# The inner layer of a four-bit feed-forward: another order of the work on TensorE and ScalarE

## The chip, the core and the metric

The kernel runs on one core of a Trainium2 chip. Five engines work from queues of their own and meet only at semaphores: TensorE (PE, matmuls and transposes, writes to PSUM), VectorE (DVE), ScalarE (ACT), GpSimd (POOL) and SyncE (SP, which issues DMAs). The metric is the device time of one launch in microseconds; lower is better. An engine works off its queue in the order in which the program wrote it: an instruction that waits for a semaphore holds up all that stand behind it on that engine, and none on another.

## The reference, cut to what matters

The model is two hybrid layers on a tensor x of shape 8 x 512 x 128. The feed-forward touched here, `_L0_ffn_ref`, is used twice, after each of the first two mixing blocks:

```python
xq   = fp4_quant_dequant(layernorm(x))          # blocks of 16 along the features
gate = einsum('bsk,nk->bsn', xq, fp4(w_gate))   # 128 -> 352
y    = einsum('bsk,nk->bsn', xq, fp4(w_up))     # 128 -> 352
h    = silu(gate) * y
x    = x + einsum('bsk,nk->bsn', fp4_quant_dequant(h), fp4(w_down))   # 352 -> 128
```

`fp4_quant_dequant` scales each block of 16 values so that its largest magnitude is 6, rounds each value to the nearest of 0, 0.5, 1, 1.5, 2, 3, 4, 6 with its sign, and multiplies by the scale again.

## The kernel before, in words

`ffn0_stages` (line 649) runs two stages per call and is called twice. The first, "fx", normalises and quantises x into `XQ`. The second, "fh" (line 795), is the one changed; in the profile its tiles are named `fh_...`. It treats G = 32 tiles j of 128 tokens; two tiles make a pair k (16 pairs), and four tiles, NT = 4, make one block m of 512 tokens (8 blocks). All tiles are f32. One pass of it takes about 115 us, and there are two passes, from 479 to 594 us and from 751 to 871 us of the span.

What happens to one tile, with the line of each instruction:

- TensorE: gate (line 822) into one of two PSUM buffers `gps`; up (line 826) into one of four buffers `ups`. Gate j may start when the silu of tile j-2 has been read out (`s.gt`), up j when `total` of tile j-4 is done (`s.tot`).
- ScalarE: `gated`, the silu of the gate (line 863).
- VectorE: `product` (line 888), `maxima` of the blocks of 16 (line 892), `scales` for the pair (lines 898 and 900), `scaled` (line 904).
- ScalarE: the magnitude times 2^22, called size (line 873).
- VectorE: `sizes` for the pair (line 909), which is the number to round against, and `total` (line 913). Adding that number to the value is what rounds it.
- GpSimd: subtracts it again (`q`, line 942) and multiplies by the scale (`hq`, line 945).
- TensorE: `turn`, three transposes of the tile (line 833) into the single buffer `tps`. ScalarE copies it out in two pieces (lines 879 and 880) to `HT`; the next turn waits for both copies (`s.ht`).
- TensorE: `down` (line 841), after the four tiles of a block have been turned: three f32 matmuls of 512 columns into the single buffer `yps`. It waits for the copies, and for VectorE to have added the previous block's result to X (`s.x`, lines 932 and 935).

Every f32 matmul appears in the profile as two MATMUL records, except a transpose, which appears as one.

The order on each engine is written out by hand. VectorE's cycle for pair k is: the products of pair k, `sizes` and both totals of pair k-1, the maxima, scales and scaled of pair k, and in every second cycle from k = 5 the addition of a finished block to X. TensorE and ScalarE go by single tiles before the change. In TensorE's cycle j come gate j+2, up j+2, turn j-4 (LAG = 4), and after every fourth turn `down`. In ScalarE's cycle j come the silu of tile j+2, the size of tile j, and the two copies of tile j-4.

Of the kernel before, what the change touches and what calls it, by code (L numbers as in the profile page):

```python
# [10 lines left out]
ACT = mybir.ActivationFunctionType  # L11
AX_X = mybir.AxisListType.X

P = 128
# [3 lines left out]
NT = T // P  # L18
N_STATE = 16
FF = 352  # L20
# [20 lines left out]
STEP = 2.0 ** 22  # L41
# [607 lines left out]
def ffn0_stages(nc, w, X):  # L649
# [7 lines left out]
    with Stage(nc, "ffn") as outer:  # L657
        XQ = outer.sb("xq", [P, B, T])
        with Stage(nc, "fx") as st:
# [8 lines left out]
            size, mag, tot, q, xq = ([st.sb(f"{n}{k}", [P, NB, FQ]) for k in range(2)] for n in ("size", "mag", "tot", "q", "xq"))  # L668
            s = st.sems("cent sq lnv rough var v1 v2 rstd amax normed above inv both xn size mag tot q xq back out")
            with st.block() as block:  # L670

                @block.tensor
                def _(pe):
                    def center(k):
                        pe.wait_ge(s.tot, max(k - RING + 1, 0))
                        for t in range(TOK):
                            n, at = 2 * k + t // NT, t % NT * P
                            m = pe.matmul(cps[k % RING][:, t * XB:(t + 1) * XB, :].rearrange("p a q -> p (a q)"), X[:, n, at:at + P], w.center[:, :], start=True, stop=True)
                        m.then_inc(s.cent, 1)

                    def back(k):
                        pe.wait_ge(s.xq, k + 1)
                        for j in range(2):
                            pe.wait_ge(s.out, max(2 * k + j - 1, 0))
                            for t in range(NT):
                                a = (j * NT + t) * XB
                                m = pe.transpose(qps[j][:, t * P:(t + 1) * P], xq[k % 2][:, a:a + XB, :].rearrange("p a q -> p (a q)"), w.ident[:, :])
                            m.then_inc(s.back, 1)

                    center(0)  # L690
                    center(1)
                    for k in range(PAIRS):
                        if k + 2 < PAIRS:
                            center(k + 2)
                        back(k)
# [98 lines left out]

        with Stage(nc, "fh") as st:
            G = NT * B
            LAG = 4
            gps = [st.ps(f"g{k}", [P, FF]) for k in range(2)]
            ups = [st.ps(f"u{k}", [P, FB, FQ]) for k in range(4)]
            tps = st.ps("t", [P, KF, P])  # L800
            yps = st.ps("y", [P, T])
            gt, q, hq = ([st.sb(f"{n}{k}", [P, FB, FQ]) for k in range(NT)] for n in ("gt", "q", "hq"))
            size, mag, tot = ([st.sb(f"{n}{k}", [P, 2, FB, FQ]) for k in range(2)] for n in ("size", "mag", "tot"))
            amax, above, inv = ([st.sb(f"{n}{k}", [P, 2, FB]) for k in range(4)] for n in ("amax", "above", "inv"))
            HT = [st.sb(f"ht{k}", [P, KF, T]) for k in range(2)]
            s = st.sems("g u gt h amax above inv xn size mag tot q hq t ht y x")
            flat = "p a q -> p (a q)"

            def real(j):

                return 0 <= j < G

            with st.block() as block:

                @block.tensor
                def _(pe):
                    def tokens(j):
                        return XQ[:, j // NT, j % NT * P:(j % NT + 1) * P]

                    def gate(j):  # L820
                        pe.wait_ge(s.gt, max(j - 1, 0))
                        pe.matmul(gps[j % 2][:, :], tokens(j), w.gate[:, :], start=True, stop=True).then_inc(s.g, 1)

                    def up(j):
                        pe.wait_ge(s.tot, max(j - 3, 0))
                        pe.matmul(ups[j % 4][:, :, :].rearrange(flat), tokens(j), w.up[:, :], start=True, stop=True).then_inc(s.u, 1)

                    def turn(j):
                        pe.wait_ge(s.hq, j + 1)
                        pe.wait_ge(s.ht, 2 * j)  # L830
                        for c in range(KF):
                            cols = min(P, FF - c * P)
                            i = pe.transpose(tps[0:cols, c, :], hq[j % NT][:, c * P // FQ:(c * P + cols) // FQ, :].rearrange(flat), w.ident[:, :])
                        i.then_inc(s.t, 1)

                    def down(m):
                        pe.wait_ge(s.ht, 2 * NT * (m + 1))
                        pe.wait_ge(s.x, m)
                        for c in range(KF):
                            rows = min(P, FF - c * P)  # L840
                            i = pe.matmul(yps[:, :], w.down[0:rows, c, :], HT[m % 2][0:rows, c, :], start=(c == 0), stop=(c == KF - 1))
                        i.then_inc(s.y, 1)

                    gate(0)
                    gate(1)
                    up(0)
                    up(1)
                    for j in range(G + LAG + 1):
                        if real(j + 2):
                            gate(j + 2)  # L850
                            up(j + 2)
                        k = j - LAG
                        if real(k):
                            turn(k)
                        if k >= NT and k % NT == 0:
                            down(k // NT - 1)

                @block.scalar
                def _(act):
                    def gated(j):  # L860
                        act.wait_ge(s.g, j + 1)
                        act.wait_ge(s.h, max(j - NT + 1, 0))
                        act.activation(gt[j % NT][:, :, :].rearrange(flat), gps[j % 2][:, :], ACT.Silu).then_inc(s.gt, 1)

                    gated(0)
                    gated(1)
                    for j in range(G + LAG):
                        if real(j + 2):
                            gated(j + 2)
                        if real(j):  # L870
                            act.wait_ge(s.xn, j + 1)
                            act.wait_ge(s.mag, max(j // 2 - 1, 0))
                            act.activation(size[j // 2 % 2][:, j % 2, :, :], ups[j % 4][:, :, :], ACT.Abs, scale=STEP).then_inc(s.size, 1)  # L873
                        k = j - LAG
                        if real(k):
                            m, t = divmod(k, NT)
                            act.wait_ge(s.t, k + 1)
                            act.wait_ge(s.y, max(m - 1, 0))
                            act.activation(HT[m % 2][:, 0:2, t * P:(t + 1) * P], tps[:, 0:2, :], ACT.Copy).then_inc(s.ht, 1)
                            act.activation(HT[m % 2][0:FF - 2 * P, 2, t * P:(t + 1) * P], tps[0:FF - 2 * P, 2, :], ACT.Copy).then_inc(s.ht, 1)  # L880

                @block.vector
                def _(dve):
# [1328 lines left out]
```

## Time and profile before

| what | before |
|---|---|
| median of 3 runs | 2394.18 us (2393.65 to 2394.51) |
| the profiled execution | 2391.51 us, its span 2389.5 us |
| mean granted TensorE clock | 0.921 |
| TensorE, matmul busy | 1911.1 us, 80% |
| VectorE busy | 1571.5 us, 66% |
| ScalarE busy | 1375.2 us, 58% |
| GpSimd busy | 1019.3 us, 43% |
| stage fh, both passes | 479 to 594 us and 751 to 871 us |

The span is the part of an execution in which the core works; the execution's own time is 2.0 us longer. Busy shares are means over stages that have different limits, so the change has to be judged from the two stretches in which stage fh runs. The granted clock is a share of 2.4 GHz; 0.5 in a stretch stands for 1.2 GHz throughout.

### The profile page before, as it was taken

How to read it: one execution, taken by the hardware profiler on the slowest of the kernel's cores; microseconds unless marked ns; L12 is line 12 of the kernel's file. 1: busy time of each engine (PE TensorE's matmuls, PEld its weight loads, DVE VectorE, ACT ScalarE, POOL GpSimd, SP SyncE). 2: the span in 40 equal slices, each digit the busy share in tenths (PEclk: the TensorE clock that was granted, in tenths of full speed). 3: DMA queues.
4: the chain of work that ended last, by engine and by line, in shares of the span. 5: the costliest groups of instructions: out<-in, count | busy, mean ns of one | idle time of the engine just before them, and what ended most of it. 6: DMA issues, size and time to landing. Idle time of an engine off the chain costs nothing. (4 is left out here: it accounts for less than half of the span.)

```text
span 2389.5 us, 36303 instructions
## 1 busy us (share of the span) xinstructions
PE 1911.1 (80%) x11731; PEld 865.0 (36%) x11731; DVE 1571.5 (66%) x2373; ACT 1375.2 (58%) x2286; POOL 1019.3 (43%) x1118
## 2 busy tenths in 40 slices
PE   4457886377774765899999999999999966599997
PEld 2113332243453421344444444444444422222222
DVE  4979995786447856777777777777777635511112
ACT  2446662343333334677666676666666533599995
POOL 0156663244004521466666666666666631500001
PEclk9769998589896987999999999999999988899999
DMA  2000000000000001111111111111111100512110
GB/s 87 0 14 0 0 0 0 1 1 1 0 1 0 1 1 52 47 55 54 53 54 56 56 56 56 56 56 56 56 56 56 50 24 8 124 41 52 46 50 36
DMA packets 71431, 84.45 MB, mean 35 GB/s; under 512 B 20545, under 2 KB 44033, under 8 KB 71169
## 3 DMA queue, kind: packets, MB, share of 16 engines
q1 hardware_dynamic: 66224, 79.80, 11.5%
q10 hardware_dynamic: 5040, 2.56, 0.4%
q8 instruction: 90, 1.47, 0.3%
q14 instruction: 77, 0.62, 0.1%
HBM read 71.95 MB, written 9.57 MB: 34 GB/s over the span
## 5 line engine op out<-in xcount | busy, mean ns | idle before, releaser
L1638 DVE SCALAR_TENSOR_TENSOR fu_kv<-fu_ps_kv,fa_vec,fu_kv 128x511 f32<-128x511 f32 x366 | 253.2, 741 | 5.6 <-ACT fu_kv L1568 4.0
L2032 ACT ACTIVATE rt_p<-rt_ps_s 128x1024 f32<-128x1024 f32 x256 | 240.3, 1042 | 25.3 <-PE rt_ps_o L1977 16.5
L1716 POOL TENSOR_TENSOR fu_p<-fu_p 128x768 f32<-128x768 f32 x64 | 116.2, 1816 | 295.2 <-PE fu_ps_n L1413 290.8
L1383 PE MATMUL fu_ps_s<-fu_qn,fu_kn 64*128 64x512 f32 (+3 forms) x1024 | 190.0, 468 | 6.1 <-ACT fu_p L1550 5.5
L1618 DVE TENSOR_REDUCE fu_nm<-fu_ps_m 128x2 f32<-128x1024 f32 x64 | 78.4, 1225 | 176.5 <-PE fu_ps_m L1406 176.5
L602 POOL TENSOR_TENSOR scan_hC<-scan_h,scan_c 128x1024 f32<-128x1024 f32 x64 | 150.7, 2354 | 82.9 <-DVE scan_h L582 82.9
L1413 PE MATMUL fu_ps_n<-fu_p,fu_vt 128*64 128x512 f32 (+3 forms) x1024 | 166.1, 445 | 0.0
L527 PE MATMUL scan_ps_y<-scan_hC,w_ident 128*128 128x512 f32 x256 | 130.3, 632 | 40.9 <-POOL scan_hC L602 24.3
L582 DVE TENSOR_TENSOR_SCAN scan_h<-scan_dA,scan_ps_b 128x1024 f32<-128x1024 f32 x64 | 146.4, 2287 | 2.2
L1977 PE MATMUL rt_ps_o<-rt_p,rt_va 128*32 128x512 f32 x1024 | 137.2, 608 | 10.0 <-ACT rt_p L2032 8.1
L1441 PE MATMUL fu_ps_kv<-w_XN,fa_wp 128*128 128x512 f32 x244 | 122.8, 626 | 17.3 <-DVE fu_cr L1611 15.3
L1383 PEld LDWEIGHTS fu_ps_s<-fu_qn,fu_kn 64*128 64x128 f32 x1024 | 82.9, 185 | 125.3 <-ACT fu_p L1572 52.1
L1966 PE MATMUL rt_ps_s<-ra_stackq,ra_stackk 48*128 48x512 bf16 x512 | 94.4, 391 | 24.6 <-PEq L73 15.5
L563 ACT ACTIVATE scan_c<-scan_ps_c 128x1024 f32<-128x1024 f32 x64 | 65.5, 1023 | 75.3 <-POOL scan_hC L602 46.3
L942 POOL TENSOR_TENSOR fh_q<-fh_tot,fh_mag 128x352 f32<-128x352 f32 x64 | 59.4, 928 | 111.3 <-DVE fh_tot L913 111.3
L1568 ACT ACTIVATE fu_kv<-fu_ps_kv,fa_vec 128x512 f32<-128x512 f32 x122 | 80.6, 686 | 38.2 <-PE fu_ps_kv L1441 34.8
L1954 POOL COPY rt_va<-ra_v 128x128 f32<-128x128 f32 x32 | 8.0, 293 | 220.3 <-PE rt_ps_o L1977 220.2
L1656 DVE SCALAR_TENSOR_TENSOR fu_og<-fu_num,fu_ow,fu_ro 128x512 f32<-128x512 f32 x64 | 84.2, 1316 | 14.4 <-issue 6.0
L559 ACT ACTIVATE scan_dA<-ssm_delta,w_decay 128x511 f32 (+1 forms) x128 | 85.0, 713 | 12.3 <-DVE scan_dA L574 11.4
L1758 POOL TENSOR_TENSOR fu_num<-fu_num,fu_sg 128x512 f32<-128x512 f32 x64 | 81.3, 1271 | 22.6 <-DVE fu_sg L1681 19.4
L873 ACT ACTIVATE fh_size<-fh_ps_u 128x352 f32<-128x352 f32 x64 | 29.9, 467 | 101.6 <-DVE fh_ps_u L904 101.6
L1574 ACT ACTIVATE fu_p<-fu_ps_s 128x512 f32<-128x512 f32 x64 | 38.2, 597 | 86.5 <-PE fu_ps_s L1391 86.5
(353 smaller groups left out, 5071.3 us busy)
## 6 DMA issues: line engine op xcount, KB each, us to landing
fu_rb<-rms_rows SPq DMA_DIRECT2D x256, 128.0 KB, 3.0
fu_ro<-rms_rows SPq DMA_DIRECT2D x128, 128.0 KB, 3.0
ra_stackq<-rope_parts SPq DMA_DIRECT2D x168, 32.0 KB
ra_stackk<-rope_parts SPq DMA_DIRECT2D x168, 32.0 KB
w_X<-in_xT SPq DMA_DIRECT2D x4, 512.0 KB
fa_wp<-in_wp SPq DMA_DIRECT2D x8, 256.0 KB
fu_cr<-ncum_rows SPq DMA_DIRECT2D x128, 3.0 KB
rope_parts<-rp_hi SPq DMA_DIRECT2D x16, 128.0 KB, 2.9
```

The costliest lines, as they stand in the source:

```text
L527: i = pe.matmul(yps[:, :], w.ident[:, :], hC[p % (BEHIND + 2)][:, j, :], start=(p == 0 and j == 0), stop=(p == PAIRS - 1 and j == 1))
L559: m = act.activation(dA[p % 2][:, j, 1:T], DL[:, n, 1:T], ACT.Exp, scale=w.decay[:, k:k + 1])
L582: dve.tensor_tensor_scan(flat[0], flat[1], flat[2], 0.0, ALU.mult, ALU.add).then_inc(s.scan, 1)
L602: pool.tensor_tensor(hC[p % (BEHIND + 2)][:, :, :], hst[p % 2][:, :, :], csb[p % 2][:, :, :], ALU.mult).then_inc(s.hC, 1)
L1383: pe.matmul(sps[:, h, at:at + T - t * P], k[head(h), t * P:(t + 1) * P], q[head(h), t * P:T], start=(at == 0), stop=False)
L1413: m = pe.matmul(nps[head(h), t * P:T], VT[b % VR][:, t, head(h)], p[:, h, :], start=(t == 0), stop=(t == 2))
L1441: pe.matmul(projected(a, j), wp[:, g, 1 + j, :], XN[:, n, :], start=True, stop=True).then_inc(s.kvp, 1)
L1638: dve.scalar_tensor_tensor(acc, projected(a, k)[:, 0:T - j], vec[:, a % GA, at:at + 1], acc, ALU.mult, ALU.add).then_inc(done, 1)
L1716: pool.tensor_tensor(tail, tail, P13[:, :, 0:3 * P], ALU.add).then_inc(s.d1, 1)
L1966: m = pe.matmul(sps[u % RING][:, e, :], stack[1][rows, 2 * q4 + i, t * P:(t + 1) * P], stack[0][rows, 2 * q4 + i, :], start=True, stop=True)
L1977: m = pe.matmul(ops[32 * j:32 * j + 32, :], va[:, t, 4 * q4 + j, :], pr[k % 2][j // 2][:, j % 2, :], start=(t == 0), stop=(t == NT - 1))
L2032: act.activation(pr[k % 2][i][:, :, :], sps[(U * n + u) % RING][:, :, :], ACT.Exp, scale=DH_B ** -0.5).then_inc(s.exp, 1)
```

## The change

TensorE and ScalarE are written in pairs of tiles, as VectorE already was, and LAG becomes 2 and counts pairs; turns therefore still come four tiles behind.

- TensorE's cycle k: for each of two tiles first its turn (of pair k-2), then its up (of pair k+1); then both gates of pair k+2; then, in every second cycle, `down`.
- ScalarE's cycle k: the two silus of pair k+1, the four copies of pair k-2, the two sizes of pair k.
- VectorE, GpSimd, all buffers, all waits and all instructions as such are the same; only their places in TensorE's and ScalarE's queues differ.

```diff
--- before.py
+++ after.py
@@ -794,7 +794,7 @@
 
         with Stage(nc, "fh") as st:
             G = NT * B
-            LAG = 4
+            LAG = 2
             gps = [st.ps(f"g{k}", [P, FF]) for k in range(2)]
             ups = [st.ps(f"u{k}", [P, FB, FQ]) for k in range(4)]
             tps = st.ps("t", [P, KF, P])
@@ -841,19 +841,20 @@
                             i = pe.matmul(yps[:, :], w.down[0:rows, c, :], HT[m % 2][0:rows, c, :], start=(c == 0), stop=(c == KF - 1))
                         i.then_inc(s.y, 1)
 
-                    gate(0)
-                    gate(1)
-                    up(0)
-                    up(1)
-                    for j in range(G + LAG + 1):
-                        if real(j + 2):
-                            gate(j + 2)
-                            up(j + 2)
-                        k = j - LAG
-                        if real(k):
-                            turn(k)
-                        if k >= NT and k % NT == 0:
-                            down(k // NT - 1)
+                    for j in range(2):
+                        gate(j)
+                        up(j)
+                    for k in range(-1, G // 2 + LAG):
+                        for e in range(2):
+                            if real(2 * (k - LAG) + e):
+                                turn(2 * (k - LAG) + e)
+                            if k >= 0 and real(2 * k + 2 + e):
+                                up(2 * k + 2 + e)
+                        for e in range(2):
+                            if real(2 * k + 4 + e):
+                                gate(2 * k + 4 + e)
+                        if k > LAG and (k - LAG) % 2 == 1:
+                            down((k - LAG) // 2)
 
                 @block.scalar
                 def _(act):
@@ -862,22 +863,23 @@
                         act.wait_ge(s.h, max(j - NT + 1, 0))
                         act.activation(gt[j % NT][:, :, :].rearrange(flat), gps[j % 2][:, :], ACT.Silu).then_inc(s.gt, 1)
 
-                    gated(0)
-                    gated(1)
-                    for j in range(G + LAG):
-                        if real(j + 2):
-                            gated(j + 2)
-                        if real(j):
-                            act.wait_ge(s.xn, j + 1)
-                            act.wait_ge(s.mag, max(j // 2 - 1, 0))
-                            act.activation(size[j // 2 % 2][:, j % 2, :, :], ups[j % 4][:, :, :], ACT.Abs, scale=STEP).then_inc(s.size, 1)
-                        k = j - LAG
-                        if real(k):
-                            m, t = divmod(k, NT)
-                            act.wait_ge(s.t, k + 1)
-                            act.wait_ge(s.y, max(m - 1, 0))
-                            act.activation(HT[m % 2][:, 0:2, t * P:(t + 1) * P], tps[:, 0:2, :], ACT.Copy).then_inc(s.ht, 1)
-                            act.activation(HT[m % 2][0:FF - 2 * P, 2, t * P:(t + 1) * P], tps[0:FF - 2 * P, 2, :], ACT.Copy).then_inc(s.ht, 1)
+                    def sized(j):
+                        act.wait_ge(s.xn, j + 1)
+                        act.wait_ge(s.mag, max(j // 2 - 1, 0))
+                        act.activation(size[j // 2 % 2][:, j % 2, :, :], ups[j % 4][:, :, :], ACT.Abs, scale=STEP).then_inc(s.size, 1)
+
+                    def turned(j):
+                        m, t = divmod(j, NT)
+                        act.wait_ge(s.t, j + 1)
+                        act.wait_ge(s.y, max(m - 1, 0))
+                        act.activation(HT[m % 2][:, 0:2, t * P:(t + 1) * P], tps[:, 0:2, :], ACT.Copy).then_inc(s.ht, 1)
+                        act.activation(HT[m % 2][0:FF - 2 * P, 2, t * P:(t + 1) * P], tps[0:FF - 2 * P, 2, :], ACT.Copy).then_inc(s.ht, 1)
+
+                    for k in range(-1, G // 2 + LAG):
+                        for part, j in ((gated, 2 * k + 2), (turned, 2 * (k - LAG)), (sized, 2 * k)):
+                            for e in range(2):
+                                if real(j + e):
+                                    part(j + e)
 
                 @block.vector
                 def _(dve):
```

## Rows read from the trace of the kernel before

**Rows 1.** Busy time by stretch: from:to, us, each engine's busy us, PEclk, DMA share, GB/s.

```profile
488.59:512.10 23.51, 17.99 (x56) 9.65 (x56) 20.72 (x44) 9.14 (x28) 13.56 (x16) 0.85 0.00 1
...
524.55:581.10 56.55, 39.60 (x140) 21.53 (x140) 48.34 (x102) 22.42 (x68) 30.47 (x36) 0.95 0.00 1
581.10:594.10 13.00, 9.45 (x25) 4.33 (x24) 2.33 (x4) 2.72 (x10) 3.38 (x4) 0.81 0.00 0
...
761.02:784.52 23.50, 17.07 (x56) 9.39 (x56) 20.70 (x44) 9.14 (x28) 13.54 (x16) 0.93 0.00 1
784.52:858.55 74.03, 53.99 (x174) 29.08 (x174) 59.18 (x125) 27.75 (x84) 37.22 (x44) 0.89 0.00 1
858.55:871.06 12.51, 8.97 (x25) 4.12 (x24) 2.32 (x4) 2.72 (x10) 3.38 (x4) 0.84 0.00 1
```

**Rows 2.** Timeline of VectorE: start us, us, engine, line, instruction [idle before <-releaser].

```profile
512.10 0.95 DVE L913 TENSOR_TENSOR fh_tot<-fh_mag,fh_ps_u 128x352 f32<-128x352 f32 x2
...
515.91 0.68 DVE L932 TENSOR_TENSOR w_X<-w_X,fh_ps_y 128x512 f32<-128x512 f32 x1
516.50 0.95 DVE L888 TENSOR_TENSOR fh_ps_u<-fh_gt,fh_ps_u 128x352 f32<-128x352 f32 x2
517.37 0.52 DVE L909 TENSOR_SCALAR fh_mag<-fh_size 128x704 f32<-128x704 f32 x1
517.92 0.95 DVE L913 TENSOR_TENSOR fh_tot<-fh_mag,fh_ps_u 128x352 f32<-128x352 f32 x2
...
520.85 0.96 DVE L904 TENSOR_TENSOR fh_ps_u<-fh_ps_u,fh_inv 128x352 f32<-128x352 f32 x2
521.72 0.52 DVE L888 TENSOR_TENSOR fh_ps_u<-fh_gt,fh_ps_u 128x352 f32<-128x352 f32 x1
523.55 0.53 DVE L888 TENSOR_TENSOR fh_ps_u<-fh_gt,fh_ps_u 128x352 f32<-128x352 f32 x1 [1.31 <-PE fh_ps_u L826]
...
524.55 0.95 DVE L913 TENSOR_TENSOR fh_tot<-fh_mag,fh_ps_u 128x352 f32<-128x352 f32 x2
```

**Rows 3.** Timeline of TensorE's matmuls in the same twelve microseconds.

```profile
518.49 0.86 PE L826 MATMUL fh_ps_u<-w_up,ffn_xq 128*128 128x352 f32 x2 [0.74 <-DVE fh_tot L913]
...
519.19 0.49 PE L833 MATMUL fh_ps_t<-w_ident,fh_hq 128*128 128x128 f32 x3
...
519.52 2.74 PE L841 MATMUL fh_ps_y<-fh_ht,w_down 128*128 128x512 f32 x6
...
522.10 0.76 PE L822 MATMUL fh_ps_g<-w_gate,ffn_xq 128*128 128x352 f32 x2
...
522.69 0.75 PE L826 MATMUL fh_ps_u<-w_up,ffn_xq 128*128 128x352 f32 x2
...
523.28 0.49 PE L833 MATMUL fh_ps_t<-w_ident,fh_hq 128*128 128x128 f32 x3
```

**Rows 4.** Timeline of ScalarE and GpSimd in the same stretch.

```profile
521.27 0.79 POOL L945 TENSOR_TENSOR fh_hq<-fh_q,fh_above 128x352 f32<-128x352 f32 x1
521.42 0.46 ACT L873 ACTIVATE fh_size<-fh_ps_u 128x352 f32<-128x352 f32 x1 [3.16 <-DVE fh_ps_u L904]
...
523.81 0.38 ACT L879 ACTIVATE fh_ht<-fh_ps_t 128x256 f32<-128x256 f32 x1
...
524.09 0.26 ACT L880 ACTIVATE fh_ht<-fh_ps_t 96x128 f32<-96x128 f32 x1
```

**Rows 5.** The line that forms the scales: durations ns min/median/max, first and last start.

```profile
L898 DVE TENSOR_SCALAR fh_above<-fh_amax x32: 186/583/592, 485.5 to 855.1; 128x44 f32<-128x44 f32 x32
```

**Rows 6.** A VectorE stall at half clock, and the down projection's durations (tile view).

```profile
L841 PE MATMUL fh_ps_y<-fh_ht,w_down x96: 590/593/1061, 507.1 to 869.7; 128*128 128x512 f32 x64, 96*128 96x512 f32 x32
...
562.33 0.53 DVE L888 TENSOR_TENSOR fh_ps_u<-fh_gt,fh_ps_u 128x352 f32<-128x352 f32 x1 [2.76 <-PE fh_ps_u L826]
```

**Rows 7.** The end of the first pass, timeline.

```profile
590.52 2.85 PE L841 MATMUL fh_ps_y<-fh_ht,w_down 128*128 128x512 f32 x6 [0.64 <-ACT fh_ht L880]
593.40 0.69 DVE L935 TENSOR_TENSOR w_X<-w_X,fh_ps_y 128x512 f32<-128x512 f32 x1 [5.61 <-PE fh_ps_y L841]
```

## The prediction

> **What bounds the kernel now.** I began with the page's 40 slices to place stage fh, then cut both passes by VectorE's totals (line 913), which mark its cycles: T(1) to T(16) are the starts of the first total in cycles 1 to 16, 15 intervals. They take 23.51 us for four, 12.45 for the next two and 56.55 for nine in pass 1, 92.51 in all, and 23.50 + 74.03 = 97.53 in pass 2; the rest up to the last addition is 13.00 and 12.51 [rows 1, 2]. In the 56.55 us VectorE is busy 48.34, TensorE 39.60, GpSimd 30.47 and ScalarE 22.42 [rows 1]. So VectorE is nearly the bound, and the question is what it waits for. The reader is to see in its timeline two kinds of cycle. One, with an addition to X, runs without a gap: 512.10 to 517.92 is 5.82. The other takes 6.63 (517.92 to 524.55), and its second product sat idle for 1.31 us until an up matmul ended [rows 2]. TensorE's timeline says why: `down` stood in the queue ahead of gate and up, from 519.52 to the next gate at 522.10 [rows 3]. Nothing in the stretch runs beside something else's end: both passes lie in series with the stages around them, so what they lose or win shows in full.
>
> **VectorE's own floor.** Its instructions and their order are not touched, so the new cycle can be put together from gapless pieces. From total to scaled 2.93 (517.92 to 520.85), scaled to product 0.87, two products to sizes 0.87 (516.50 to 517.37), sizes to total 0.55: 5.22, taken as 5.23. An addition puts 0.59 in (515.91 to 516.50), and 5.82 is what was measured [rows 2]. The last interval has an addition and no products, so ScalarE's size ends it: about 5.0. Additions stand in cycles 5, 7, 9, 11, 13 and 15. Fifteen intervals: 9 x 5.23 + 5 x 5.82 + 5.0 = 81.2 us. Against 92.5 and 97.5 that is 11.3 and 16.3 us, if no other engine ever comes late. That is what has to be checked, engine by engine.
>
> **Does TensorE come late?** Start to start at the full clock: gate or up 0.59 (522.10, 522.69, 523.28), three transposes 0.33 (519.19 to 519.52), down 2.58 (519.52 to 522.10) [rows 3]. Two cycles need 4 x 0.33 + 8 x 0.59 + 2.58 = 8.6 us of the floor's 11.05, so it has room. The places: a waiting up starts 0.57 after the total (517.92 to 518.49) [rows 2, 3]. In an odd cycle (T its total): up T+0.57, turn 1.16, up 1.49, gates 2.08 and 2.67, free at 3.26. Now `down`. It waits for the previous block's addition, which stands at T+3.80 in the same VectorE cycle and lasts 0.68: down starts at T+4.53, not 3.26. This wait is harmless in the old order and is met in the new one in cycles 5, 7, ... 15. Behind it in the queue stand the next turn and up. They get TensorE at T+4.53+2.58 = T+7.11, which is 1.29 us into the next cycle (T'). From there: turn 1.29, up 1.62; the second turn needs both copies of the first. Turn to copy is 0.53, copy to copy 0.28, the second lasts 0.26 [rows 3, 4], and with about 0.15 for the signal the second turn starts at T'+2.51, the second up at 2.84 and ends at 2.84+0.75 = 3.6 [rows 3]. VectorE wants the first tile at T'+3.80 and the second at T'+4.23. So the up is in time by 0.6 us, and before it was late by 1.31. The gates follow at T'+3.4 and 4.0 for silus that are wanted a whole cycle later; two pairs ahead, they can no longer make the product wait. The 0.6 us is the thinnest cover in the change on this engine: longer down, turns or copies by more than that come back one for one, six or seven times a pass.
>
> **Does ScalarE come late?** VectorE's sizes needs both magnitudes by T'+4.66. The first starts 0.57 after scaled (520.85 to 521.42), at T'+3.50 [rows 2, 4], the second 0.43 later; it lasts 0.46 and ends at 4.4, 0.25 us early. In the even cycle the second tile's copies end at about T'+3.6 (turn 2.51, then the 1.07 above), just when the first size could start, which eats some 0.1 of the 0.25. Everything else on ScalarE has microseconds. GpSimd needs 4.14 us after a total until both tiles are out (521.27 + 0.79, from 517.92) of a cycle of 5.23 [rows 4], and a turn wants them a cycle later. No DMA, SyncE instruction or buffer is involved.
>
> **A contention that could move.** The scales instruction of 128 x 44 elements takes 583 ns at the median and 186 at least, the first of a pass, when GpSimd is still idle [rows 5]. Both start from the total, and stay in the same phase in the new order, so I keep the 583; 0.4 us per cycle below that would need GpSimd elsewhere. The Trainium skill (GPSIMD Engine Reference, section Specifications) says that GpSimd's SBUF interfaces are shared with VectorE and contended by instructions in a two-port mode. By that rule a closer cycle would speak against the change if the 704-element sizes came to lie beside GpSimd. The trace's phases answer it: sizes at T+4.66, GpSimd done at T+4.14, so by the rule and by the row the sum is the same, with 0.5 us of margin.
>
> **Clock.** The stretches were granted 0.95 and 0.89 of full speed [rows 1]. A stall that fell at half clock was 2.76 instead of 1.31 [rows 6]. TensorE idles 12.45 - 8.6 = 3.8 us per two cycles now and 2.4 in the new order, in pieces of 0.3, 0.9 and 1.3. I take full clock in the loop, and count falls in the range: one lengthens the chain behind down by what the two stalls differ by, 2.76 - 1.31 = 1.45 us, less the 0.6 of cover, so costs about 0.9.
>
> **Start and end.** The second product still waits for the first two gates and ups, whatever their order, so I count the start at nothing. At the end, before, `down` of block 6 ran after the last totals, in front of four turns. Now it starts at T(15)+4.53, 0.5 us ahead of T(16). But TensorE has stood idle for some four microseconds by then (no up and no gate is left in cycle 15, and by the working above the second turn is done 5 to 5.5 us after T(14), down starts 9.8 after it), and half-clock matmuls of down last 1061 ns instead of 593 [rows 6], so it may run to T(16)+3.9. Then three turn intervals of 1.24, 1.15 from turn to down, 2.88 down to addition (590.52 to 593.40), 0.69 [rows 7]: 12.3. With the full clock it is about 10.5, the last tile from GpSimd at T(16)+4.14 then being the limit. I take 12.3: 0.7 and 0.2 us gained; the other end is 2.5 and 2.0.
>
> **Sum.** 11.3 + 16.3 + 0.7 + 0.2 = 28.5 us. Profiled execution 2391.5 - 28.5 = 2363.0. The runs shown have their median 2.7 above the profiled one, so 2365.7.
>
> **Rivals.**
>
> *A. The wait for the addition leaves a stall.* The chain addition, down, turn, two copies, turn, up has six signals, and I priced each from one row. If they add 1 to 2 us, VectorE still waits 0.4 to 1.4 us in every even cycle, 6 a pass, 12 in all: 5 to 17 us back, time 2371 to 2383, about 2376. For it: 0.6 us is thin, and this wait was never met in the trace of before. Against it: every link is in a row, and the old chain is regular to 0.01 us.
>
> *B. The size comes late.* If the copies of the second turn run into the sizes by 0.3 us more than I have, sizes waits 0.15 to 0.3 in the even cycles and the 0.46 us silu in front of it comes to matter: 12 to 28 cycles by 0.2 is 2 to 6 us, about 2370.
>
> *C. Slower, by the clock.* TensorE now stands idle 1.3 us right ahead of its longest work, and again 0.9. If the clock stays at 1.2 GHz there, down takes 5.16, the turns and up double, and the second product comes at about T'+7.7 instead of 4.23: 3.5 us in each of 12 even cycles, 42 us, more than the loops' 27.6 that the order brings. That gives 2366 + 42 = 2408. It decides as soon as two of three chains run at half clock (27.6 / 42). Against it: before, the idle pieces were longer and the clock was 0.95 and 0.89. The Trainium skill (TensorE: Matmul & The Clock Gate, section A second HAM failure mode) describes a kernel in which frequent short idles between groups of matmuls make the clock go up and down; by that rule falls would not vanish here. The trace shows such falls, at most in a part of the stalls.
>
> *D. No change.* The wait would have to move whole to another engine; the work of ScalarE and GpSimd, 22.42 and 30.47 of 56.55, speaks against it [rows 1].
>
> **How the numbers follow.** Forecast 0.66, A 0.14, B 0.12, C 0.04, D 0.02, and 0.02 for a gain above the range, from a vanished contention or both tails at full clock. Forecast alone: 2361 (tails at full clock, 28.5 + 3.6 = 32.1, and a little more) to 2370 (five falls of the clock at 0.9 us). With A's likelier half the range is 2360 to 2378. About 0.2%, 4.8 us, is what a measurement of this kernel can tell from no change. Faster 0.94 (forecast, B, A, the extra), same 0.02, slower 0.04.
>
> **What would show it.** In the trace after: VectorE's intervals from total to total alternating 5.23 and 5.82 with no product waiting for up; down starting about 0.06 us after line 932's addition ends, and not with the last gate; size (line 873) directly behind scaled for both tiles, 0.43 apart; the 15 intervals 81 us in both passes, alike. Idle before line 888 of over 0.1 us in even cycles says A; idle before line 909 says B; down records above 1 us in the loop say C.

## The result and the profile after

The changed kernel takes 2370.41 us (median of 4 runs, 2367.84 to 2371.97) against 2393.91 us before (4 runs, 2392.79 to 2394.51): a ratio of 0.9900, with a 95% interval of 0.9886 to 0.9914. The forecast was 2365.7 us, with 2360 to 2378 as its range. The profiled execution took 2367.84 us, its span 2366.0, against 2391.51 and 2389.5.

| from the profiled executions, us | before | forecast | after |
|---|---|---|---|
| pass 1: first gate to T(1) | 9.56 | 9.56 | 8.86 |
| pass 1: 15 intervals | 92.51 | 81.2 | 81.80 |
| pass 1: end | 12.99 | 12.3 | 16.24 |
| pass 2: first gate to T(1) | 9.69 | 9.69 | 9.56 |
| pass 2: 15 intervals | 97.53 | 81.2 | 80.97 |
| pass 2: end | 12.51 | 12.3 | 12.76 |
| both passes | 234.8 | 206.3 | 210.2 |

Here and below an interval runs from the first total of one VectorE cycle to that of the next, and the end of a pass from T(16) to the end of its last addition. Both passes together became 24.6 us shorter and everything else 1.1 us longer, which makes the span's 23.5.

The stretches of the changed kernel, each pass's 15 intervals and its end, which answer to [rows 1] (columns as there):

```profile
488.29:570.09 81.80, 63.55 (x229) 35.77 (x230) 79.11 (x170) 36.97 (x112) 50.77 (x60) 0.97 0.00 1
570.09:586.33 16.24, 12.71 (x24) 4.90 (x23) 2.32 (x4) 2.18 (x8) 3.38 (x4) 0.64 0.00 0
753.20:834.17 80.97, 63.56 (x229) 35.71 (x230) 78.90 (x170) 37.00 (x112) 50.75 (x60) 0.96 0.00 1
834.17:846.93 12.76, 9.22 (x24) 3.78 (x23) 2.33 (x4) 2.18 (x8) 3.38 (x4) 0.85 0.00 1
```

VectorE is now busy 79.11 of 81.80 us: it has become the bound of the loop. Its timeline, an even cycle and an odd one (... stands for rows left out), beside [rows 2]:

```profile
526.82 0.95 DVE L915 TENSOR_TENSOR fh_tot<-fh_mag,fh_ps_u 128x352 f32<-128x352 f32 x2
...
530.62 0.95 DVE L890 TENSOR_TENSOR fh_ps_u<-fh_gt,fh_ps_u 128x352 f32<-128x352 f32 x2
...
532.04 0.95 DVE L915 TENSOR_TENSOR fh_tot<-fh_mag,fh_ps_u 128x352 f32<-128x352 f32 x2
...
535.83 0.68 DVE L934 TENSOR_TENSOR w_X<-w_X,fh_ps_y 128x512 f32<-128x512 f32 x1
536.43 0.95 DVE L890 TENSOR_TENSOR fh_ps_u<-fh_gt,fh_ps_u 128x352 f32<-128x352 f32 x2
...
537.84 0.95 DVE L915 TENSOR_TENSOR fh_tot<-fh_mag,fh_ps_u 128x352 f32<-128x352 f32 x2
```

The two products of a cycle follow each other in one record, with no idle time in front of either: 5.22 and 5.80 us. Two rows of the table remain to be read, the ends. Both `down` of the end of pass 1 are here, then both of pass 2:

```profile
569.73 5.46 PE L841 MATMUL fh_ps_y<-fh_ht,w_down 128*128 128x512 f32 x6 [4.13 <-DVE w_X L934]
...
574.98 0.56 PE L833 MATMUL fh_ps_t<-w_ident,fh_hq 128*128 128x128 f32 x3
...
580.25 5.35 PE L841 MATMUL fh_ps_y<-fh_ht,w_down 128*128 128x512 f32 x6 [0.63 <-ACT fh_ht L876]
585.64 0.69 DVE L937 TENSOR_TENSOR w_X<-w_X,fh_ps_y 128x512 f32<-128x512 f32 x1 [9.73 <-PE fh_ps_y L841]
...
833.81 4.86 PE L841 MATMUL fh_ps_y<-fh_ht,w_down 128*128 128x512 f32 x6 [4.14 <-DVE w_X L934]
...
843.36 2.85 PE L841 MATMUL fh_ps_y<-fh_ht,w_down 128*128 128x512 f32 x6 [0.63 <-ACT fh_ht L876]
```

TensorE stood idle for 4.13 us ahead of `down` of block 6 and ran it in 5.46 us, at half clock; in pass 1 the last `down` came at half clock as well (5.35 against 2.85), and the mean granted clock of that end is 0.64.

Below, each experiment's median stands beside runs of the kernel before that were measured together with it, and kernels are compared by these ratios; a pair of figures in brackets is the lowest and highest run, or, behind a ratio, its 95% interval.

### The profile page after: what moved, and what is told of

Read it like the earlier page. It is cut to its first block and busy times, and to the rows that moved or that the text cites. A ratio compares the mean times of both kernels' runs of the same rounds, so it can differ in the third digit from the quotient of the medians.

```text
span 2366.0 us, 36303 instructions
## 1 busy us (share of the span) xinstructions
PE 1907.3 (81%) x11731; PEld 863.8 (37%) x11731; DVE 1564.1 (66%) x2373; ACT 1375.2 (58%) x2286; POOL 1021.3 (43%) x1118
## 3 DMA queue, kind: packets, MB, share of 16 engines
q8 instruction: 90, 1.47, 0.3%
## 5 line engine op out<-in xcount | busy, mean ns | idle before, releaser
L1968 PE MATMUL rt_ps_s<-ra_stackq,ra_stackk 48*128 48x512 bf16 x512 | 94.7, 393 | 24.6 <-PEq L73 15.5
L535 PE MATMUL scan_ps_b<-ssm_bc,scan_selbc 96*128 (+1 forms) x128 | 40.7, 401 | 56.9 <-DMA scan_selbc<-in_selbc 56.3
```

Source lines behind the costliest of these rows:

```text
L1968: m = pe.matmul(sps[u % RING][:, e, :], stack[1][rows, 2 * q4 + i, t * P:(t + 1) * P], stack[0][rows, 2 * q4 + i, :], start=True, stop=True)
```

## Experiments

**1. TensorE's order alone.** ScalarE keeps its order by single tiles (silu of j+2, size of j, copies of j-4).

```diff
-                    for k in range(-1, G // 2 + LAG):
-                        for part, j in ((gated, 2 * k + 2), (turned, 2 * (k - LAG)), (sized, 2 * k)):
+                    for j in range(G + 4):
+                        # silu of j + 2, size of j, copies of j - 4, as before
```

> TensorE in the new order, ScalarE in the old one by single tiles. Theory (the two orders need each other: the second turn of a pair stands in front of the second up, and waits for the first turn's copies): in the old order ScalarE makes those copies only behind the size of the pair's first tile, T+3.9 to 4.4, so turn comes at T+4.5 and the up ends at T+5.6 instead of T+3.6; a cycle from total to total is then about 6.65 us instead of 5.23 or 5.82, the 15 intervals of a pass about 100 us (before 92.5 and 97.5, after 81.8 and 81.0), and the time about 2404 us, slower than before. Rival (moving down to the end of TensorE's cycle and the gates ahead is what brings the gain, ScalarE's order adds the 0.3 to 0.5 us of late sizes in cycles without an addition): about 2378 us.

2417.92 us (2414.16 to 2421.16) beside 2393.02, ratio 1.0108 (1.0081 to 1.0134). The 15 intervals take 105.7 and 104.9 us, about half of them 6.75 or 7.68. ScalarE's, TensorE's and VectorE's timeline in one of 6.80, close to the first kind:

```profile
525.21 0.46 ACT L874 ACTIVATE fh_size<-fh_ps_u 128x352 f32<-128x352 f32 x1 [2.92 <-DVE fh_ps_u L905]
...
525.61 0.39 ACT L880 ACTIVATE fh_ht<-fh_ps_t 128x256 f32<-128x256 f32 x1
525.89 0.26 ACT L881 ACTIVATE fh_ht<-fh_ps_t 96x128 f32<-96x128 f32 x1
...
526.30 0.52 PE L833 MATMUL fh_ps_t<-w_ident,fh_hq 128*128 128x128 f32 x3
...
526.65 0.76 PE L826 MATMUL fh_ps_u<-w_up,ffn_xq 128*128 128x352 f32 x2
...
527.52 0.53 DVE L889 TENSOR_TENSOR fh_ps_u<-fh_gt,fh_ps_u 128x352 f32<-128x352 f32 x1 [0.72 <-PE fh_ps_u L826]
```

That is the chain expected: the size, then the copies, the second turn, the second up, and only then the product. The 6.75 was expected as 6.65; the intervals of 7.5 and more were not, and with them the time is 14 us above the 2404 expected. They come with a mean clock of 0.85 in the loop; that the clock alone makes them was not tested. The rival (2378) falls.

**2. ScalarE's order alone.** TensorE keeps gate, up, turn by single tiles, with `down` after every fourth turn.

```diff
-                    for k in range(-1, G // 2 + LAG):
-                        # turn, up, turn, up; both gates; down
+                    for j in range(G + 4 + 1):
+                        # gate and up of j + 2, turn of j - 4, down, as before
```

> ScalarE in the new order, TensorE in the old one by single tiles with down in the middle. Theory (the orders need each other): the silus and copies of both tiles stand in front of the sizes, and the second gate and second turn come late, behind down above all; sizes end about T+5.2 in cycles with an addition or without down, and T+7.9 in those with down, so intervals of about 5.8 and 8.4 us, 107 us a pass, about 2415 us, clearly slower than before. Rival (late sizes were half of the matter, and ScalarE's order alone takes them away): a little faster than before, about 2388 us, with the stall of the second product behind down still 1.3 us.

2426.84 us (2425.48 to 2428.41) beside 2393.02, ratio 1.0147 (1.0123 to 1.0171). Intervals of 6.9 and 10.1 us in pass 1 (116.3 for 15), of about 7.0 and 8.4 in pass 2 (110.1): the 8.4 was expected, the 6.9 to 7.0 had been put at 5.8, and the 10.1 comes with a lower clock again (0.82 against 0.87) and five `down` of 3.9 to 4.1 us where pass 2 has 2.74. In a cycle of pass 1 with `down`:

```profile
518.96 3.89 PE L841 MATMUL fh_ps_y<-fh_ht,w_down 128*128 128x512 f32 x6
...
523.48 0.46 ACT L863 ACTIVATE fh_gt<-fh_ps_g 128x352 f32<-128x352 f32 x1 [6.90 <-PE fh_ps_g L822]
...
524.14 0.53 DVE L889 TENSOR_TENSOR fh_ps_u<-fh_gt,fh_ps_u 128x352 f32<-128x352 f32 x1 [3.00 <-PE fh_ps_u L826]
...
526.36 0.53 DVE L910 TENSOR_SCALAR fh_mag<-fh_size 128x704 f32<-128x704 f32 x1 [1.69 <-ACT fh_size L868]
```

ScalarE, which now does nothing else before the second silu, waits 6.90 us for its gate behind `down`, and VectorE waits twice. So each half alone makes the kernel slower, by 1.1 and 1.5%, and the two together 1.0% faster: they are one change, and there is no share of the gain for either.

**3. Down in front of the gates.** Only TensorE's `down` moves, to between the ups and the gates.

```diff
+                        if k > LAG and (k - LAG) % 2 == 1:
+                            down((k - LAG) // 2)
                         for e in range(2):
                             if real(2 * k + 4 + e):
                                 gate(2 * k + 4 + e)
-                        if k > LAG and (k - LAG) % 2 == 1:
-                            down((k - LAG) // 2)
```

> The changed kernel with down in front of the two gates of its cycle instead of behind them. Theory (last in the cycle matters because down waits for the addition until T+4.5 and holds up whatever stands behind it): the gates come at T'+2.5, the silus behind them hold back the first turn's copies and the sizes, and the even cycles grow by about 2.2 us, five a pass, so the time is about 2392 us; at least 0.6 us a cycle, 2376 us. Rival (gates are wanted a whole cycle later, so their place is free): 2370 us, intervals unchanged.

2387.32 us (2380.79 to 2390.61) beside 2393.02, ratio 0.9977 (0.9965 to 0.9989): most of the gain is gone. The 15 intervals take 94.0 and 94.8 us; after a `down` that waits for an addition they are 7.99 in nine of ten. Forecast was 2.2 us more than 5.22, or 7.4. What was missing:

```profile
526.07 4.51 PE L841 MATMUL fh_ps_y<-fh_ht,w_down 128*128 128x512 f32 x6 [2.27 <-DVE w_X L934]
...
530.42 1.35 PE L822 MATMUL fh_ps_g<-w_gate,ffn_xq 128*128 128x352 f32 x4
...
531.21 1.06 ACT L864 ACTIVATE fh_gt<-fh_ps_g 128x352 f32<-128x352 f32 x2 [5.37 <-PE fh_ps_g L822]
...
532.80 0.53 DVE L890 TENSOR_TENSOR fh_ps_u<-fh_gt,fh_ps_u 128x352 f32<-128x352 f32 x1 [1.65 <-PE fh_ps_u L826]
...
534.07 0.53 DVE L890 TENSOR_TENSOR fh_ps_u<-fh_gt,fh_ps_u 128x352 f32<-128x352 f32 x1 [0.74 <-PE fh_ps_u L826]
```

Without the gates to do, TensorE idles 2.27 us until the addition instead of 1.09, and `down` then takes 4.51 us instead of 2.8, mostly at half clock. The first such `down` of pass 1 had the same 2.27 us of idle time ahead of it and still took 2.82; the interval after it is the tenth, 6.30. So the idle time alone does not say whether the clock falls.

**4. The gates one pair ahead.** They stand first in TensorE's cycle, in front of the turns and ups.

```diff
+                        for e in range(2):
+                            if k >= 0 and real(2 * k + 2 + e):
+                                gate(2 * k + 2 + e)
                         # turn, up, turn, up as before
-                        for e in range(2):
-                            if real(2 * k + 4 + e):
-                                gate(2 * k + 4 + e)
```

> The changed kernel with the gates one pair ahead instead of two: they stand first in TensorE's cycle, just before the turns and ups of the same cycle. Theory (two pairs ahead takes the silus, and the copies behind them, off the chain behind down): after a down, gates come at T'+1.3 and 1.9, the first turn's copies wait for the second silu until T'+3.1, the second up ends at T'+4.9 against 4.2, and the sizes end at 5.7 against 4.7: 0.7 to 1.05 us in each of five even cycles a pass, 7 to 10 us, about 2379 us; intervals after a down of 5.9 to 6.3 instead of 5.22. Rival (the pairing alone carries the gain, gates are early enough one pair ahead): intervals unchanged, 2370 us.

2389.58 us (2385.79 to 2392.43) beside 2395.44, ratio 0.9975 (0.9965 to 0.9986), 94.0 us for the 15 intervals in both passes, and 7.99 again in eight of ten (6.29 in the others). I had overlooked that this is the same queue as in experiment 3: `down`, both gates, turn. "Gates two pairs ahead" and "down last" are one statement, and this run repeats the one above; the 5.9 to 6.3 us expected left the clock out.

**5. Is it the place or the clock?** Experiment 3, with three matmuls that nobody reads in each of the five waits of a pass for the addition:

```diff
                         pe.wait_ge(s.ht, 2 * NT * (m + 1))
+                        for i in range(3 if 0 < m < B - 2 else 0):
+                            pe.matmul(tps[:, :, :].rearrange("p c o -> p (c o)")[:, 0:FF], w.ident[:, :], w.gate[:, :], start=True, stop=True)
                         pe.wait_ge(s.x, m)
```

> Down in front of the gates and the additions where they were, with three matmuls of 352 columns, whose results nobody reads, in each of the five waits of a pass for the addition (blocks 1 to 5). Theory (the cycles of 7.99 us are made of the place, 1.1 us, and of down at half clock behind 2.3 us of idle time, 1.7 us): down runs at full clock and the intervals after it become 6.3 us, 15 of them about 87 us instead of 94 to 95, about 2374 us. Rival (the clock has no part, it is the place alone): intervals of 7.99 stay, 2387 us.

2377.44 us (2375.20 to 2377.88) beside 2393.78, ratio 0.9927 (0.9907 to 0.9947). Every interval after a waiting `down` is 6.23, the 15 take 86.95 and 86.09. TensorE's timeline (line 839 is the three unread matmuls):

```profile
523.55 2.04 PE L839 MATMUL fh_ps_t<-w_gate,w_ident 128*128 128x352 f32 x6
525.69 2.85 PE L843 MATMUL fh_ps_y<-fh_ht,w_down 128*128 128x512 f32 x6
528.37 1.35 PE L822 MATMUL fh_ps_g<-w_gate,ffn_xq 128*128 128x352 f32 x4
```

So of the 2.77 us (7.99 - 5.22) the place costs 1.01 and the half clock behind the idle time 1.76. With more work on TensorE the kernel is faster than in experiment 3 (ratio 0.9927 against 0.9977).

**6. Down in front of the gates, without its wait.** Experiment 3 with VectorE's additions moved from the odd cycles to the even ones (the start of the closing loop, which adds what is left, changes with it and is left out here):

```diff
-                        if k >= 5 and k % 2 == 1:
+                        if k >= 4 and k % 2 == 0:
```

> Down in front of the gates, and the additions moved to the even cycles, so that down no longer waits for one. Theory (down's place matters only through that wait: behind it TensorE stands idle 2.3 us when the gates come after down, against 1.1 to 1.3 when they come before): intervals of 5.22 and 5.82 in both passes, 82 us for 15, as with the additions moved alone, about 2366 us. Rival (down's 2.6 us in front of the gates are too much for the cycle whatever it waits for): even cycles above 6 us remain, 2375 us or more.

2363.36 us (2361.05 to 2368.45) beside 2393.78, ratio 0.9878 (0.9856 to 0.9900). The 15 intervals take 81.87 and 81.85 us, in 5.22 and 5.82 but for one of 6.1 in each pass, behind `down` of block 0:

```profile
485.56:567.43 81.87, 66.51 (x238) 36.66 (x238) 79.19 (x169) 38.03 (x114) 50.84 (x60) 0.98 0.00 1
```

With no wait for the addition `down` may stand on either side of the gates; its place matters through that wait alone.

**7. The changed kernel with the additions in even cycles.** The same edit of VectorE's queue in the changed kernel.

> The changed kernel, with VectorE's additions of a finished block moved by one cycle, from the odd cycles 5, 7, ... to the even ones 4, 6, ...; down then finds its wait for the previous addition already met and starts with the last gate at T+3.3. Theory (in the loop the wait for the addition is covered; it costs only at the end of a pass, where it puts down of block 6 behind 4 us of idle time, at half clock): the 15 intervals stay at 81 us in both passes, the end of a pass falls from 16.2 and 12.8 to about 9.0 to 11.5 us, time about 2364 us. Rival (the wait costs in the loop too): the intervals fall by over 1 us a pass. Rival (no effect, the end is set by the last tile alone): 2370 us.

2367.60 us (2366.96 to 2370.16) beside 2393.02, ratio 0.9896 (0.9873 to 0.9919):

```profile
488.18:570.04 81.86, 65.19 (x238) 37.25 (x238) 79.18 (x170) 37.62 (x114) 50.89 (x60) 0.98 0.00 1
570.04:581.99 11.95, 7.79 (x15) 3.05 (x15) 2.23 (x4) 1.63 (x6) 3.38 (x4) 0.56 0.00 0
750.50:832.35 81.85, 66.68 (x237) 37.76 (x237) 79.16 (x169) 37.08 (x112) 50.87 (x60) 0.96 0.00 1
832.35:843.00 10.65, 6.29 (x17) 2.54 (x15) 2.23 (x4) 2.18 (x8) 3.40 (x4) 0.84 0.00 1
```

The loop doesn't gain by it: the wait for the addition was covered, as forecast. (Pass 2 took 0.9 us more, by one interval of 6.05 behind `down` of block 0.) The ends fall by 4.3 and 2.1 us. The run's time shows none of it, 0.9896 against 0.9900: in these two profiles the forgetting attention stage, which the edit does not touch, took 1041.7 us here and 1035.6 in the changed kernel.

**8. The ends of a pass, filled.** The changed kernel with ten gate matmuls that nobody reads (the expectation says nine): six before `down` of block 6, one each before turns 29, 30 and 31 and the last `down`. The places from which it is called are left out here.

```diff
+                    def filler(n):
+                        pe.wait_ge(s.gt, G)
+                        for i in range(n):
+                            pe.matmul(gps[i % 2][:, :], tokens(0), w.gate[:, :], start=True, stop=True)
```

> The changed kernel with nine more gate matmuls, whose results nobody reads, put where TensorE stands idle at the end of a pass: six in front of down of block 6, one each in front of turns 29, 30 and 31 and of the last down. Theory (the end of a pass is long because both downs run at half clock behind idle time): both run at full clock, down records near 0.59 us, and the end falls from 16.2 and 12.8 to about 10.6 us in both passes, time about 2362 us. Rival (the waits set the end, the clock does not matter): the ends stay, or grow by the fillers, 2370 to 2373 us.

2363.31 us (2363.28 to 2366.31) beside 2391.89, ratio 0.9880 (0.9860 to 0.9900). Both ends:

```profile
569.09:579.82 10.73, 9.57 (x32) 4.22 (x30) 2.33 (x4) 2.18 (x8) 3.39 (x4) 1.00 0.00 0
827.65:838.38 10.73, 9.56 (x32) 4.22 (x30) 2.33 (x4) 2.18 (x8) 3.39 (x4) 1.00 0.00 1
```

10.73 us at a clock of 1.00, where 16.24 and 12.76 had been at 0.64 and 0.85. Filled ends with the additions in even cycles, here eight matmuls: one before turn 29, four before turn 30, two before turn 31 and one before the last `down`:

> The additions moved to even cycles as before, and eight filler matmuls at the end of a pass (one before turn 29, four before turn 30, two before turn 31, one before the last down). Theory of the clock: the last down runs at full clock, ends of 11.95 and 10.65 us become about 9.2 in both passes, time about 4 us below the same kernel without fillers (2367.6), 2363 us. Rival (fillers stand in the way of the turns): ends of 11 us or more.

2359.82 us (2354.16 to 2363.01) beside 2391.89, ratio 0.9857 (0.9833 to 0.9880), ends of 8.95 and 9.84 us at 1.00, where 9.2 was expected. In pass 2 `down` of block 6, which stands ahead of T(16) here and has no filler in front, took 4.43 us instead of 2.84.

**9. The scales instruction.** The block maxima go to unused columns of PSUM buffers of the tiles (`ups`). The lines that write and read them are left out here.

```diff
-            ups = [st.ps(f"u{k}", [P, FB, FQ]) for k in range(4)]
+            uraw = [st.ps(f"u{k}", [P, 32, FQ]) for k in range(4)]
+            ups = [u[:, 0:FB, :] for u in uraw]
+            amax = [uraw[2 * k][:, 24:27, :].rearrange("p a q -> p (a q)")[:, 0:2 * FB].rearrange("p (t f) -> p t f", f=FB) for k in range(2)]
```

> The changed kernel, with the block maxima kept in PSUM beside the tile that they come from instead of in SBUF; the scales instruction of 128 x 44 elements then reads PSUM. Theory (its 583 ns instead of 186 is a contention with GpSimd for SBUF): it falls to about 0.2 us, the interval without an addition from 5.22 to about 4.83, with some 0.2 us given back in even cycles, where the sizes then end last (0.17 us of cover so far): about 9 to 11 us in all, 2360 us. Rival (the 0.4 us is a latency of the short chain itself, or PSUM costs as much): the instruction stays near 0.58, intervals unchanged, 2370 us.

2354.77 us (2351.89 to 2357.44) beside 2391.89, ratio 0.9840 (0.9819 to 0.9861), more than the 9 to 11 us expected: the loops became 9.4 us shorter (76.66 and 76.75 for 15 intervals), and the ends 3.7 (12.42 and 12.84). These are the usual ends of this order, as experiment 11 shows, and the 3.7 us are not put down to the instruction. The instruction in the changed kernel and, below it, in this one (durations min/median/max):

```profile
L900 DVE TENSOR_SCALAR fh_above<-fh_amax x32: 185/582/592, 485.3 to 831.0; 128x44 f32<-128x44 f32 x32
```

```profile
L902 DVE TENSOR_SCALAR fh_above<-fh_ps_u x32: 203/204/205, 486.3 to 818.7; 128x44 f32<-128x44 f32 x32
...
529.20 0.53 DVE L913 TENSOR_SCALAR fh_mag<-fh_size 128x704 f32<-128x704 f32 x1
```

The interval without an addition that follows no `down` is 4.85 instead of 5.22; after one it is 5.09. The last line is such a cycle: sizes starts 1.09 us after the first product (528.11) instead of 0.86, because the second size is late. That is the thin cover of rival B, used up by the quicker cycle, and 0.24 us of 0.37 are given back there.

What the instruction had waited for shows in the changed kernel's timeline:

```profile
561.50 0.79 POOL L947 TENSOR_TENSOR fh_hq<-fh_q,fh_above 128x352 f32<-128x352 f32 x1
561.75 0.58 DVE L900 TENSOR_SCALAR fh_above<-fh_amax 128x44 f32<-128x44 f32 x1
```

It starts 0.24 us after GpSimd's `hq` and ends 0.04 us after it. So it does in all 30 cycles in which `hq` runs beside it, with durations from 576 to 592 ns; in the first cycle of each pass, with GpSimd idle, it takes 185 and 188. With its input in PSUM it starts at the same place and ends 0.33 us ahead of `hq`. Its output was in SBUF throughout.

**10. All three.** Additions in even cycles, filled ends, maxima in PSUM.

> Additions in even cycles, fillers at the end, and the block maxima in PSUM. Theory: the intervals fall by 0.39 us each with nothing given back, since down no longer stands in the way (4.83 and 5.43, 15 of them about 76 us), ends of about 9.2 us: 11 to 12 us below the kernel with additions in even cycles and fillers, about 2352 us. Rival (with a cycle of 4.83 the next engine is the bound: GpSimd's 4.14 us or the wait of a turn for copies): intervals of about 5.1, 2360 us.

2346.85 us (2345.64 to 2348.21, 5 runs) beside 2391.89, ratio 0.9807 (0.9791 to 0.9824), against 0.9900 for the change alone: the fastest version here, and 5 us below the 2352 expected. The intervals are 4.85 and 5.44 (the last 4.62), and nothing comes late:

```profile
487.43:563.49 76.06, 64.09 (x240) 36.55 (x240) 73.47 (x169) 37.19 (x114) 50.90 (x60) 1.00 0.00 1
563.49:572.45 8.96, 8.20 (x29) 4.36 (x29) 2.24 (x4) 1.63 (x6) 3.40 (x4) 1.00 0.00 0
```

**11. The changed kernel again.**

> The changed kernel itself once more, on the chip and in the call of the one above, to part what belongs to the layer from what moves elsewhere. Theory: intervals of 5.22 and 5.82 again, 15 of them 81 to 82 us, while the ends of the passes vary with the clock between 10.6 and 16.3 us and the forgetting attention (about 1036 to 1042 us) by some us, so that the time lies between 2366 and 2373 us. Rival (the ends are fixed by the order): 16.2 and 12.8 us again.

2369.60 us (2368.84 to 2374.17) beside 2395.44, ratio 0.9904 (0.9883 to 0.9924):

```profile
488.17:570.02 81.85, 63.55 (x229) 35.76 (x230) 79.17 (x170) 36.96 (x112) 50.76 (x60) 0.97 0.00 1
570.02:586.24 16.22, 12.69 (x24) 4.88 (x23) 2.32 (x4) 2.17 (x8) 3.38 (x4) 0.64 0.00 0
753.14:834.15 81.01, 63.54 (x229) 35.73 (x230) 78.96 (x169) 37.00 (x112) 50.77 (x60) 0.96 0.00 1
834.15:846.88 12.73, 9.19 (x24) 3.80 (x23) 2.33 (x4) 2.18 (x8) 3.38 (x4) 0.86 0.00 1
```

Against my expectation the ends repeat to 0.03 us, half-clock `down` included: the rival, ends fixed by the order, foretold these two executions. But the order alone does not fix them. From the turn of tile 24 on, TensorE's order and waits are the same in experiments 3, 4, 5, 9 and 11 as in the changed kernel, and of these twelve ends three took 16.1 to 16.2 us and nine 12.3 to 12.8. In experiment 5 it was pass 2 that had the long one:

```profile
574.32:586.89 12.57, 9.04 (x24) 3.73 (x23) 2.32 (x4) 2.18 (x8) 3.38 (x4) 0.87 0.00 0
...
839.13:855.22 16.09, 12.56 (x24) 4.84 (x23) 2.32 (x4) 2.17 (x8) 3.38 (x4) 0.64 0.01 2
```

So the same end is 12.3 to 12.8 us or 16.1 to 16.2, according to where the clock is granted; what decides that, no run here tells. What also moved is the forgetting attention stage, 1040.5 us here and 1035.6 in the first profile, outside the change.

## Why the prediction was right, point by point

- **The bound and its floor: right.** VectorE's gapless cycle was put at 5.23 and 5.82, the last interval at 5.0; measured 5.22, 5.82 and 4.98. Both passes came out within 0.8 us of each other although they had been 5 us apart, since the stalls at half clock, as in [rows 6], are gone with all others.
- **TensorE in time by 0.6 us: right in kind, 0.2 us too generous.** The timeline behind a waiting `down`, beside [rows 3]:

```profile
525.64 2.82 PE L841 MATMUL fh_ps_y<-fh_ht,w_down 128*128 128x512 f32 x6 [1.09 <-DVE w_X L934]
528.29 0.49 PE L833 MATMUL fh_ps_t<-w_ident,fh_hq 128*128 128x128 f32 x3
528.62 0.76 PE L826 MATMUL fh_ps_u<-w_up,ffn_xq 128*128 128x352 f32 x2
529.51 0.52 PE L833 MATMUL fh_ps_t<-w_ident,fh_hq 128*128 128x128 f32 x3
529.86 0.76 PE L826 MATMUL fh_ps_u<-w_up,ffn_xq 128*128 128x352 f32 x2
```

  With T' = 526.82 the turns start at 1.47 and 2.69 and the second up at 3.04, where I had 1.29, 2.51 and 2.84. `down` starts 0.15 us after the addition's end (524.81 + 0.68), not 0.06, and lasts 2.65 start to start, not 2.58. The up ends at T'+3.80, 0.4 us ahead of the second product. Once it did not hold, in the interval after `down` of block 0 in pass 1: 6.04 instead of 5.22, with a product 0.54 us late, after an up and gates at half clock. That is the one fall of the clock that the loops paid for, 0.8 us, where the range had put such a fall at 0.9.
- **ScalarE in time: right.** Sizes never waited; experiment 9 measured the cover by using it up.
- **The contention: right.** The scales instruction stayed at 582 ns, as forecast. That "0.4 us per cycle below that would need GpSimd elsewhere" was too narrow: experiment 9 left GpSimd where it was and moved the instruction's input, 582 ns with it in SBUF and 204 in PSUM. The Trainium skill (GPSIMD Engine Reference, section Specifications) says that VectorE's instructions in a two-port mode contend with GpSimd for SBUF. The two durations and the ends 0.04 us behind `hq` agree with that; in which mode the instruction runs, no row shows.
- **The clock in the loop: right; rival C: not there.** Idle pieces of 1.09 us ahead of `down` left it at 2.8 us. Experiments 3 and 5 show how near it was: with 2.27 us of idle time instead the clock fell in nine of ten, and with that time filled in none.
- **The end of a pass: the term that was mis-sized.** "Then three turn intervals of 1.24, 1.15 from turn to down, 2.88 down to addition" was to make 12.3 us in both passes. `down` of block 6 did start 0.36 us ahead of T(16), at half clock, as said, but freed TensorE at T(16)+4.9 in pass 1 instead of +3.9, and the last `down` took 5.39 to its addition instead of 2.88. With 0.4 us more for the turns between, that makes 16.24 us, 3.9 more than forecast; pass 2 took 0.5 more. I had taken the full clock for the last `down` from the old order, and the range's other end was the better case only, not the worse. Experiment 8 shows it is the clock: 10.73 us in both passes when TensorE is kept busy, beside the 10.5 forecast for the full clock. The 12.3 itself is near what nine of twelve such ends took, 12.3 to 12.8 us (experiment 11); what was missing is the other case.
- **The start: forecast at nothing,** gained 0.70 and 0.13 us.
- **The sum.** Forecast 28.5 us: loops 27.6, ends 0.9. Measured in the profiles: loops 27.3, ends -3.5 (longer than before), starts 0.8, elsewhere -1.1, in all 23.5. Of the 5.0 us missing in the profiles (4.7 in the medians), 4.4 are the ends.
- **Luck.** Starts and elsewhere, both counted at nothing, nearly cancel. And 2370.4 us lies just above what the forecast alone was to give (2361 to 2370); it lies inside the stated range because that was widened for rival A, which did not come. By the time alone it could have been rival B (2370) or five falls of the clock. Only the trace says that it was the forecast's loop and a longer end.
- **Rivals.** A and B cost nothing in the changed kernel: no product waited for an up in the loops but the one above, and sizes never waited. D is out.

## What to carry to other kernels

Put the floor of the engine that is nearly the bound together from stretches in which it runs without a gap, then walk the other engines' queues through it and write down for each wait by how much it is in time; those covers (0.4 us here, and the second size's, forecast at some 0.2) say what the next change will run into. An order written out on two engines is one change when each waits for the other within a cycle: half of it can be worse than none. And price each matmul behind an idle stretch twice, at either clock: the ends of a pipelined stage, where an engine waits, deserve that more than the loop.

## What the runs showed of the hardware that I had not expected

- A VectorE instruction on 44 elements per partition took 582 ns beside a busy GpSimd, ending each time 0.04 us after GpSimd's own instruction, 185 ns with GpSimd idle, and 204 ns beside a busy GpSimd when its input lay in PSUM: 0.38 us less in each of 30 cycles.
- TensorE at the full clock after 1.1 us of idle time in the loop, mostly at 1.2 GHz after 2.27 us, in nine of ten (`down` 2.8 and 4.51 us); three unread matmuls in that gap gave back 1.76 us a cycle.
- The half-clock ends of the passes repeated to 0.03 us in two executions of one program, in which another stage differed by 4.9 us; in another program with the same order there, the long end was that of the other pass.
